# Order of VectorE's work in a Strassen-like gate/up stage: splits of later weights behind the products' sums, and the seam to the down projection

## The chip, the cores and the metric

One core of one Trainium2 chip. The metric is the device time of one execution in microseconds (us); a lower time is better. Engines: PE is TensorE, DVE is VectorE, ACT is ScalarE, POOL is GpSimd, SP is SyncE, which issues all DMAs.

## The reference

Input x of 2 x 512 x 512 passes through a Mamba-2 layer with a gated MLP, a layer norm, a BitLinear feed-forward with ternary weights, and a second layer norm. The change touches the gated MLP:

```python
h2 = rmsnorm(h, ln2_w)
mlp = silu(h2 @ gate_w.T) * (h2 @ up_w.T) @ down_w.T      # INTER = 1792, D_MODEL = 512
return res + mlp
...
def _bitlinear(x, w):
    scale = jnp.mean(jnp.abs(w))
    q = jnp.round(jnp.clip(w / (scale + EPS), -1.0, 1.0))
    return x @ (q * scale).T
```

## The kernel before

All products keep fp32 accuracy with single-pass matmuls: each operand is split into a high part (ScalarE copies it to the rounded type) and a low part (VectorE or GpSimd subtracts the high part from the original), and three products of parts are summed in PSUM.

Gate and up are computed for both batches together with seven products instead of eight (a 2x2 block scheme of the Strassen-Winograd kind). For each of 14 tiles f of 128 inner columns, PE runs six matmuls for each product: p6, then p4 of the tile before, p5, p7 and p3 (p1 and p2 of most tiles ran earlier, under the scan; for the tiles 11, 12 and 13 they are "fillers" within tiles 1, 3 and 5). VectorE forms the sums: line 1245 (p6: u_t), line 1251 (p5: v_t), line 1257 (p7: adds v_t, written to p5's PSUM bank), line 1263 (p3: c12), line 1269 (m1: silu(c12) times the sum, which frees p5's bank) and lines 1276 and 1279 (p4). PE's p4 waits for line 1257 (c22_ready). Lines 1105 and 1114 are VectorE's splits of weights for later: 1105 for a filler ("ga" loads), 1114 for a22 two tiles on ("gb" loads). ScalarE's silu of c12 is line 1000.

Then comes the down projection: for each of 14 tiles f PE multiplies act (split at line 1010 on ScalarE and line 1313 on VectorE) by the down weights (split at line 845 on ScalarE and line 1304 on VectorE, two tiles for each load "dn"), into four accumulators, the PSUM banks psB that p5's last tiles used.

Meanwhile VectorE quantizes the ternary weights of the feed-forward in halves (lines 1327 and 1329).

All weights pass through one buffer raw with three slots. SyncE issues the loads in the order of the list LOADS; load n waits until load n - 3 has been used by all its readers:

```python
for n, (kind, *at) in enumerate(LOADS):
    if n >= RAW_SLOTS:
        for used in raw_used(n - RAW_SLOTS):
            sp.wait_ge(*used)
...
if n in TERN:
    return [(tern_ready, TERN.index(n) + 1)]
```

Around the seam the list reads gb 13, ternary 2, dn 0, dn 1, dn 2, ternary 3, dn 3, ternary 4. Each engine walks the same written-out list SCHEDULE and carries out the part of each step that is its own, strictly in order. build_schedule writes it.

Of the kernel before, what the change touches and what calls it, by code (L numbers as in the profile page):

```python
# [37 lines left out]
FM = 1792 // P  # L38
# [10 lines left out]
def build_schedule():  # L49

    steps, loads = [], []

    def load(kind, *which):
        loads.append((kind, *which))
        return ("load", len(loads) - 1)
# [98 lines left out]
    def ternary():  # L154

        which = tern.pop(0)
        halves = 1 if which == ("qdn", FF // 2) and FF % 2 else 2
        return [load(*which)], [("quant", which, i) for i in range(halves)]

    filler = {1: NPRE, 3: NPRE + 1, 5: NPRE + 2}  # L160
    halves = []
    for f in range(FM):
        steps.append(("p6", f))
        if f >= 1:
            steps += [("m1", f - 1), ("p4", f - 1)]
        if f + 1 < FM:
            steps.append(("gsplit", f + 1))
        if f + 2 < FM:
            steps.append(load("gb", f + 2))
        if f == FM - 1:  # L170
            steps.append(load("dn", 0))
        if f + 1 in filler:
            steps.append(load("ga", filler[f + 1]))
        steps.append(("p5", f))
        if f == FM - 1:
            steps += [("act", 0, 0), ("act", 0, 1)]
        if f in filler:
            steps.append(("p1", filler[f]))
        steps.append(("p7", f))
        if f < NPRE:  # L180
            steps.append(("silu0", f))
        steps.append(("p3", f))
        if f in filler:
            steps.append(("p2", filler[f]))
        if sums:
            steps.append(load(*sums.pop(0)))
        if f == 7:
            steps.append(("scales",))
        if f in (8, 10, 12):
            loads_now, halves = ternary()  # L190
            steps += loads_now
        if f >= 8:
            steps.append(halves.pop(0))
    steps += [("p4", FM - 1), load("dn", 1), ("m1", FM - 1)]

    for f in range(FM):
        if f % 2 == 0 and f // 2 + 2 < FM // 2:
# [3 lines left out]
        if f % 2 == 0:  # L201
            loads_now, halves = ternary()
# [5 lines left out]
    for f in range(FM):  # L208
# [7 lines left out]
        if f in (4, 6, 8, 10, 12):  # L216
            loads_now, halves = ternary()
# [7 lines left out]
    for b in range(NB):  # L225
        for f in range(FF):
# [9 lines left out]
            if tern and f in (2, 4):  # L236
                loads_now, halves = ternary()
# [11 lines left out]


SCHEDULE, LOADS = build_schedule()
RAW_SLOTS = 3
DN_EARLY = 9
# [1438 lines left out]
```

## Time and profile before

| | |
|---|---|
| median of 3 runs | 496.98 us (496.71 to 497.38) |
| the profiled execution, its own time | 495.74 us |
| its span, first to last instruction | 494.0 us |
| PE busy | 472.2 us, 96% |
| VectorE busy | 318.7 us, 65% |
| ScalarE busy | 236.4 us, 48% |
| GpSimd busy | 215.5 us, 44% |
| mean granted TensorE clock | 0.996 |

The engines run side by side, so the busy times overlap. What lies between the span and the device time is start and end of the execution.

### The profile page before, as it was taken

The numbers are of one execution on the slowest core, as the hardware profiler recorded it, in microseconds if no ns is written. First come the engines' busy times: TensorE is split into PE (matmuls) and PEld (weight loads), VectorE is DVE, ScalarE is ACT, GpSimd is POOL, SyncE is SP. The second block draws the span as 40 slices with busy tenths as digits, with TensorE's granted clock in tenths as the row PEclk, the third lists the DMA queues.
The fourth block names the chain that finished last, engine by engine and source line by source line (L and its number), as shares of the span: only waits on it lengthen the run. The fifth ranks groups of instructions, "written<-read, shape, count | busy, mean of one in ns | idle before, by whom it ended". The sixth has DMA issues, their size and how long they took to land.

```text
span 494.0 us, 6223 instructions
## 1 busy us (share of the span) xinstructions
PE 472.2 (96%) x2104; PEld 375.8 (76%) x2104; DVE 318.7 (65%) x518; ACT 236.4 (48%) x444; POOL 215.5 (44%) x242
## 2 busy tenths in 40 slices
PE   8998999989989979999999899999999999999995
PEld 7776677766757868888788778888888888888884
DVE  3793786735788856777998889865957513411223
ACT  5887767776556667455343244233806430033200
POOL 5835476626773596767877000010004432133321
PEclk9999999999999999999999999999999999999998
DMA  7631022013202415342322257510300000200001
GB/s 244 204 108 49 37 86 65 21 40 110 83 26 85 158 56 192 130 161 95 129 97 81 79 198 227 171 45 2 127 21 1 0 0 1 85 2 0 2 14 71
DMA packets 14431, 40.80 MB, mean 83 GB/s; under 512 B 2368, under 2 KB 2368, under 8 KB 14400
## 3 DMA queue, kind: packets, MB, share of 16 engines
q1 hardware_dynamic: 14400, 40.41, 24.1%
q8 instruction: 17, 0.28, 0.2%
q14 instruction: 14, 0.11, 0.1%
HBM read 38.30 MB, written 2.10 MB: 82 GB/s over the span
## 4 chain that ended last, share of the span: by engine, by line
PE 78%; DVE 12%; issue 4%; ACT 3%; POOL 1%; POOLq 0%; DVEq 0%; ACTq 0%
PE psA L1619 8%; PE psA L1620 8%; PE psA L1408 6%; PE psA L1410 6%; PE psB L1629 4%; PE psB L1628 4%; PE psA L1414 3%; PE psA L1416 3%; PE psA L1598 3%; PE psA L1594 3%; PE psA L1597 3%; DVE xbc L1168 2%; PE psB L1594 2%; PE psB L1598 2%; PE psB L1597 2%
## 5 line engine op out<-in xcount | busy, mean ns | idle before, releaser
L1619 PE MATMUL psA<-xT_h,q_gu 128*128 128x512 f32 x176 | 70.1, 398 | 0.0
L1620 PE MATMUL psA<-xT_l,q_gu 128*128 128x512 f32 x176 | 69.1, 393 | 0.0
L669 POOL TENSOR_SCALAR var<-mv 128x1 f32<-128x1 f32 x16 | 4.9, 304 | 128.8 <-DVE mv L1060 128.7
L1031 ACT ACTIVATE gate_t<-psA 128x512 f32<-128x512 f32 x22 | 13.1, 597 | 75.1 <-PE psA L1620 75.1
L816 POOL TENSOR_TENSOR int_l<-prod_t,int_h 128x512 fp32r<-128x512 f32 x22 | 28.7, 1305 | 45.7 <-ACT int_h L1036 45.7
L1360 DVE TENSOR_TENSOR prod_t<-gate_t,psA 128x512 f32<-128x512 f32 x22 | 15.2, 689 | 51.7 <-PE psA L1620 48.6
L727 POOL TENSOR_TENSOR beta<-wsum,beta 128x512 fp32r<-128x512 f32 x28 | 36.1, 1310 | 25.0 <-ACT beta L892 25.0
L1619 PEld LDWEIGHTS psA<-xT_h,q_gu 128*128 128x128 f32 x176 | 33.1, 188 | 8.2
L1620 PEld LDWEIGHTS psA<-xT_l,q_gu 128*128 128x128 f32 x176 | 33.1, 188 | 7.4
L1629 PE MATMUL psB<-q_dn,int_l 128*128 128x512 f32 x88 | 34.3, 389 | 0.0
L1628 PE MATMUL psB<-q_dn,int_h 128*128 128x512 f32 x88 | 34.2, 389 | 0.0
L1000 ACT ACTIVATE c<-c 128x512 f32<-128x512 f32 x14 | 8.9, 633 | 51.1 <-DVE c L1263 51.1
L1396 PE MATMUL psA<-xT_h,win_h 128*128 128x512 f32 x80 | 32.7, 409 | 0.0
L1397 PE MATMUL psA<-xT_l,win_h 128*128 128x512 f32 x80 | 31.4, 392 | 0.0
L1168 DVE SCALAR_TENSOR_TENSOR xbc<-psA,convw_sb,xbc 128x511 f32<-128x511 f32 (+2 forms) x36 | 26.8, 746 | 0.8
L1329 DVE SCALAR_TENSOR_TENSOR q<-raw,scl,qtmp 128x512 fp8e4<-128x512 f32 x33 | 25.7, 779 | 1.2
L1010 ACT ACTIVATE act_hl<-act 128x512 fp32r<-128x512 f32 x28 | 16.9, 623 | 17.7 <-PE psB L1598 12.4
L1367 DVE SCALAR_TENSOR_TENSOR x<-psB,scl,x 128x512 f32<-128x512 f32 x8 | 6.0, 751 | 26.5 <-PE psB L1629 26.5
L1408 PE MATMUL psA<-xT_h,beta 128*128 128x512 f32 x56 | 22.4, 399 | 0.3 <-DVE act L1279 0.3
L1313 DVE TENSOR_TENSOR act_hl<-act,act_hl 128x512 fp32r<-128x512 f32 x28 | 19.1, 687 | 4.9 <-ACT act_hl L1010 4.9
L1410 PE MATMUL psA<-xT_l,beta 128*128 128x512 f32 x56 | 21.9, 391 | 0.0
L1401 PE MATMUL psA<-xT_h,win_l 128*128 128x512 f32 x80 | 21.9, 395 | 0.0
(251 smaller groups left out, 1359.1 us busy)
## 6 DMA issues: line engine op xcount, KB each, us to landing
raw<-in_f_gu_t SPq DMA_DIRECT2D x22, 512.0 KB, 3.5
raw<-in_w_gu_t SPq DMA_DIRECT2D x14, 512.0 KB, 4.1
raw<-in_f_dn_t SPq DMA_DIRECT2D x10, 512.0 KB, 3.3
raw<-in_w_gu_t SPq DMA_DIRECT2D x14, 256.0 KB, 2.7
raw<-in_w_dn_t SPq DMA_DIRECT2D x7, 512.0 KB, 3.3
raw<-in_w_in_t SPq DMA_DIRECT2D x5, 512.0 KB, 4.4
x<-in_hidden SPq DMA_DIRECT2D x8, 256.0 KB, 5.3
out<-x SPq DMA_DIRECT2D x8, 256.0 KB, 2.0
```

The lines of the kernel that those rows point to most:

```text
L727: nc.gpsimd.tensor_tensor(beta[:, f % 2, 1, cols], wsum[:, f % 2, cols], beta[:, f % 2, 0, cols].bitcast(F32), ALU.subtract).then_inc(gb_l ...
L816: nc.gpsimd.tensor_tensor(int_l[:, f, :], prod_t[:, n % 2, :], int_h[:, f, :].bitcast(F32), ALU.subtract).then_inc(int_ready, 1)
L1168: add = nc.vector.scalar_tensor_tensor(out=xbc[b][:, j, back:L], in0=bank_a(job)[:, 0:L - back], scalar=convw_sb[:, j, TAPS - 1 - back:TAP ...
L1329: last = nc.vector.scalar_tensor_tensor(out=q8[:, f, cols], in0=raw[:, n % RAW_SLOTS, cols], scalar=scl[:, 6 + w:7 + w], in1=qtmp[:, cols] ...
L1396: nc.tensor.matmul(ps, sh, mh, start=i == 0, stop=False)
L1397: nc.tensor.matmul(ps, sh, ml, start=False, stop=False)
L1408: nc.tensor.matmul(ps, weights[:, 0, chunk(k)], high[:, k, :], start=opens and k == 0, stop=False, skip_group_check=not opens)
L1410: nc.tensor.matmul(ps, weights[:, 0, chunk(k)], low[:, k, :], start=False, stop=False, skip_group_check=not opens)
L1619: nc.tensor.matmul(ps, w, seq(xT_h, k, b), start=k == 0, stop=False)
L1620: done = nc.tensor.matmul(ps, w, seq(xT_l, k, b), start=False, stop=k == KD - 1)
L1628: nc.tensor.matmul(ps, int_h[:, f, chunk(c)], q_dn[:, f, :], start=f == 0, stop=False)
L1629: done = nc.tensor.matmul(ps, int_l[:, f, chunk(c)], q_dn[:, f, :], start=False, stop=f == FF - 1)
```

## The change

The list of steps is written in another order within the seven products; no step is added or dropped. For every tile the sum of the fifth product stands ahead of the gb load's step. A filler's ga step moves from ahead of the fifth product to behind the third. In the last tile, act's first tile and the step of dn 0 move behind the seventh product, act's second tile behind the third product. At the end m1 comes ahead of p4 and of dn 1, and the last half of ternary weights 2 is quantized behind dn 1 instead of directly behind the third product. The order of the loads among themselves stays.

```diff
         if f + 1 < FM:
             steps.append(("gsplit", f + 1))
+        steps.append(("p5", f))
         if f + 2 < FM:
             steps.append(load("gb", f + 2))
-        if f == FM - 1:
-            steps.append(load("dn", 0))
-        if f + 1 in filler:
-            steps.append(load("ga", filler[f + 1]))
-        steps.append(("p5", f))
-        if f == FM - 1:
-            steps += [("act", 0, 0), ("act", 0, 1)]
         if f in filler:
             steps.append(("p1", filler[f]))
         steps.append(("p7", f))
         if f < NPRE:
             steps.append(("silu0", f))
+        if f == FM - 1:
+            steps += [("act", 0, 0), load("dn", 0)]
         steps.append(("p3", f))
+        if f == FM - 1:
+            steps.append(("act", 0, 1))
+        if f + 1 in filler:
+            steps.append(load("ga", filler[f + 1]))
         if f in filler:
             steps.append(("p2", filler[f]))
...
-        if f >= 8:
+        if 8 <= f < FM - 1:
             steps.append(halves.pop(0))
-    steps += [("p4", FM - 1), load("dn", 1), ("m1", FM - 1)]
+    steps += [("m1", FM - 1), ("p4", FM - 1), load("dn", 1), halves.pop(0)]
```

## Rows read from the trace of the kernel before

**Rows 1.** The page's first part: busy us, share of the span, instructions.

```profile
PE 472.2 (96%) x2104; PEld 375.8 (76%) x2104; DVE 318.7 (65%) x518; ACT 236.4 (48%) x444; POOL 215.5 (44%) x242
```

**Rows 2.** PE's waits from 176 to 494 us: total us, times, longest.

```profile
PE psA L1408 <- DVE psB L1257: 2.1, 2, 1.2
PE psB L1594 <- DVE act L1269: 1.2, 1, 1.2
...
```

**Rows 3.** Timeline at the first wait: start, duration (us), engine, line, operation.

```profile
183.09 0.39 PE L1416 MATMUL psA<-tT_h,beta 128*128 128x512 f32 x1
184.34 0.47 PE L1408 MATMUL psA<-tT_h,a 128*128 128x512 f32 x1 [0.86 <-DVE psB L1257]
...
189.96 0.40 PE L1408 MATMUL psA<-xT_h,beta 128*128 128x512 f32 x1
...
181.06 1.72 DVE L1105 TENSOR_TENSOR alpha<-raw,alpha 128x512 fp32r<-128x512 f32 x1
182.71 0.68 DVE L1251 TENSOR_TENSOR v_t<-psB,u_t 128x512 f32<-128x512 f32 x1
183.49 0.70 DVE L1257 TENSOR_TENSOR psB<-psA,v_t 128x512 f32<-128x512 f32 x1
...
186.81 0.69 DVE L1279 TENSOR_TENSOR act<-psA,act 128x512 f32<-128x512 f32 x1
```

**Rows 4.** Timeline of VectorE at the seam to the down projection.

```profile
279.48 1.22 DVE L1304 TENSOR_TENSOR dn_early<-raw,dn_early 128x1024 fp32r<-128x1024 f32 x1
...
281.21 1.28 DVE L1313 TENSOR_TENSOR act_hl<-act,act_hl 128x512 fp32r<-128x512 f32 x2
...
283.02 0.68 DVE L1263 TENSOR_TENSOR c<-psA,v_t 128x512 f32<-128x512 f32 x1
...
284.13 0.75 DVE L1329 SCALAR_TENSOR_TENSOR q<-raw,scl,qtmp 128x512 fp8e4<-128x512 f32 x1
...
286.25 1.22 DVE L1304 TENSOR_TENSOR dn_early<-raw,dn_early 128x1024 fp32r<-128x1024 f32 x1
287.38 0.68 DVE L1269 TENSOR_TENSOR act<-psB,c 128x512 f32<-128x512 f32 x1
289.28 1.23 DVE L1304 TENSOR_TENSOR dn_early<-raw,dn_early 128x1024 fp32r<-128x1024 f32 x1 [1.22 <-ACT dn_early L845]
290.42 0.69 DVE L1313 TENSOR_TENSOR act_hl<-act,act_hl 128x512 fp32r<-128x512 f32 x1
```

**Rows 5.** Timeline of PE, ScalarE and SyncE's queue at the same place.

```profile
281.62 0.40 PE L1416 MATMUL psA<-xT_h,beta 128*128 128x512 f32 x1
283.26 0.47 PE L1408 MATMUL psA<-tT_h,a 128*128 128x512 f32 x1 [1.24 <-DVE psB L1257]
...
288.12 0.50 PE L1594 MATMUL psB<-dn_early,act_hl 128*128 128x512 f32 x1 [1.21 <-DVE act L1269]
...
291.69 0.39 PE L1594 MATMUL psB<-dn_early,act_hl 128*128 128x512 f32 x1
...
283.73 0.63 ACT L1000 ACTIVATE c<-c 128x512 f32<-128x512 f32 x1 [5.22 <-DVE c L1263]
...
288.19 1.06 ACT L845 ACTIVATE dn_early<-raw 128x1024 fp32r<-128x1024 f32 x1 [2.87 <-DMA raw<-in_w_dn_t]
...
284.91 0.33 SPq L645 DMA_DIRECT2D raw<-in_w_dn_t  x1
```

**Rows 6.** Stretches: us, busy of five engines, granted clock, DMA share, GB/s.

```profile
2.00:3.00 1.00, 0.59 (x3) 0.59 (x4) 0.00 (x0) 0.06 (x1) 0.88 (x3) 1.00 0.76 285
4.00:5.00 1.00, 1.00 (x6) 1.00 (x5) 0.00 (x0) 0.95 (x4) 0.49 (x2) 1.00 0.71 207
6.00:7.00 1.00, 1.00 (x12) 1.00 (x11) 0.71 (x2) 0.13 (x1) 0.17 (x1) 1.00 0.78 233
490.00:491.00 1.00, 0.00 (x0) 0.00 (x0) 0.32 (x1) 0.00 (x0) 0.92 (x2) 0.66 0.00 0
```

**Rows 7.** Timeline of PE at the end of the span.

```profile
487.76 0.39 PE L1629 MATMUL psB<-q_dn,int_l 128*128 128x512 f32 x1
```

## The prediction

> **What bounds the kernel now.** I read the page first. TensorE (PE) is busy for 472.2 us, 96% of the span [rows 1], so a change of order on VectorE can only act through the moments in which PE stands still. The list of PE's waits comes next, from the first of the seven products to the end of the span [rows 2]: two waits for the sum that line 1257 writes, 2.1 us together, and one of 1.2 us for line 1269. Apart from one wait of less than 0.4 us near 246 us, that is all. After 288.12 us PE waits for nothing to the end of the span. So a delay or a gain at the start of the down stage reaches the end undiminished: nothing behind it has slack to swallow or to refill.
>
> The timeline at the first of these waits [rows 3] shows that the last matmul of the second tile's sixth product starts at 183.09 us, and the fourth product's first not before 184.34. The latter wants the sum of tile 0's seventh product (line 1257), which VectorE starts at 183.49, directly behind the fifth's sum (line 1251, 182.71). That one stood behind a split of 1.72 us at line 1105. Six matmuls start 0.23 us apart, a product takes 1.4 us, so the fifth product had been out since about 179.3: VectorE's order made the wait. The other two waits are of the same kind and stand at the seam to the down stage [rows 4, 5]: the split of the first down weights (279.48) and two splits of act (281.21) precede the last tile's seventh sum, and PE restarts at 283.26; then the split of the second down weights (286.25) precedes line 1269 (287.38), which frees the bank that the down product's fourth accumulator wants, and PE restarts at 288.12.
>
> The third thing to read is SyncE's row [rows 5]. It issues the third load of down weights (dn 2) at 284.91. The buffer raw has three slots, and this load takes the slot of ternary weights 2; their second half is read by line 1329, which runs 0.75 us from 284.13, to 284.88 [rows 4]. So this load waits for VectorE's quantization, and its place in VectorE's order sets when the load goes out. ScalarE takes the load up at 288.19, 3.28 us after its issue, VectorE splits it at 289.28, and only then comes act's split for tile 2, at 290.42, done at 291.11. PE starts tile 2 of down at 291.69. The margin is 0.6 us.
>
> **The change part by part.** No instruction is added or removed; PE's, GpSimd's and SyncE's orders of instructions stay as they are (the list of loads keeps its order), VectorE's and ScalarE's change.
>
> First part, tiles 0 to 12. The sum of the fifth product goes ahead of the split at line 1114, and the filler's split at line 1105, with ScalarE's copy that feeds it, goes behind the third product. For tile 0, the seventh product is out at about 180.7, and with line 1105 gone VectorE can start line 1257 at 181.06, where that split started. It ends by 181.8, before PE asks for it at 183.09 + 0.23 = 183.32. Gain: 184.34 - 183.32 = 1.02 us, and 0.08 more because the first matmul after a wait takes 0.47 us against 0.39 us: **1.1 us**. The split at line 1105 now waits for ScalarE behind the third product's silu, to about 184.0. It costs from 0.7 us (line 1251's size, the same 128x512) to 1.72 us, so it ends at 184.7 to 185.7. Queued behind it on VectorE are the next tile's u_t (0.6), m1 (0.6) and the two steps of p4 (0.7 and 0.7, line 1279 last): done between 187.4 and 188.4. For these PE waits with tile 1's third product, which would now start at 189.96 - 1.02 = 188.94. Hidden behind PE's products, with 0.5 us left at the dear end; without that cover it would cost 1 us. The filler's own product comes at about 186.1, also later than the split. The other two fillers (13 and the one before it) have the same pattern without a wait of before, so 0. The splits of line 1114 feed a product two tiles on: 0.
>
> Second part, tile 13. I keep the clock of before and subtract the 1.1 at the end. PE ends the seventh product at about 280.6 (six matmuls, 1.4 us, ahead of 282.0, where the last product ends). Line 1257 runs at once, to 281.4. PE wants it at 281.62 + 0.23 = 281.85, instead of 283.26: the second wait goes, 1.4 us. Then VectorE: first split of act 281.25, first down split 281.85, which holds it 1.13 us (279.48 to the next, less the later spacing), so the third product's sum at 283.0, as before (283.02). ScalarE's silu follows 0.7 later (283.73 before), and only behind it, by its new order, the copy for the second tile of act: 284.25 to 284.85. VectorE stands idle from 283.7 to 284.9. Then its second split of act, 284.9; m1 (line 1269) 285.5 to 286.2; p4's two steps 286.1 and 286.8; the second down split 287.4; the quantization 288.55, then line 1329 at 289.05 to **289.8**.
>
> What this does to PE is in two steps. The down product reaches its fourth accumulator at 281.85 + 1.4 + 9 x 0.23 = 285.3 and waits for m1 to 286.25: 1.9 us earlier than 288.12, and the first and second tile of down end at 289.8. Here the third tile should begin. But the load of dn 2 now goes out at 289.8 instead of 284.9, **4.9 us later**. With the same 3.28 us to ScalarE, 1.09 to VectorE's split, 1.14 to act's split and 0.69 for it, that is 293.1, 294.2, 295.35, 296.05. ScalarE's copy of act for tile 2 stands behind the down copy in its order, so it can't slip ahead. PE starts tile 2 at 296.15 instead of 291.69: **4.4 us later**, after standing still for 6.1 us; 0.1 more for the restart (0.50 against 0.39) makes 4.5. Queued behind on SyncE are the loads of ternary weights 3 and dn 3, which shift by as much, as does VectorE's later work; PE has shifted by nearly the same, so the next tiles keep their margins and cost nothing.
>
> Third part, the clock. The waits of [rows 2] are 1.2 us at most, and the mean clock stays at 0.996 over the span. What a longer pause does shows at the end of the span: the last matmul starts at 487.76 [rows 7], and in the stretch from 490 to 491 us the granted clock is 0.66 on average [rows 6]: it fell about 2.2 us after PE's last work, from 2.4 to 1.2 GHz. After 6.1 us of idling I expect the same fall. What a fall costs: at the start of the span PE runs transposes of one shape, 3 in 0.59 us, then 6 per us, and 12 per us in the stretch from 6 to 7 us [rows 6]; so half speed lasted between 2.6 and 4.6 us (the clock's column says 1.00 there, the rate doesn't). Half of that is lost: 1.3 to 2.3 us. I take **1.6 us**, a little under the middle, since 5.0 us is only the last moment at which the slow rate is seen; the term is an estimate. The Trainium skill (TensorE: Matmul & The Clock Gate, "What's actually happening") has the throttled state as the default, which activity releases; the row at the end of the span agrees. By that rule the time is 502.0 us, and 500.4 us if this pause is an exception to it.
>
> **Sum.** -1.1 + 4.5 + 1.6 = +5.0 us. The profiled execution took 495.74 us, of which 494.0 are the span and 1.7 lie around it; it would take 500.7. The median of the runs is 1.24 above it, so 496.98 + 5.0 = **502.0 us**.
>
> **The rivals.**
> A: the load is late as above, but the clock doesn't fall. For it: PE's waits of up to 1.2 us passed without a fall. Against it: the fall 2.2 us after the last matmul. -1.1 + 4.5 = +3.4: 500.4 us.
> B, on the other side: faster, because dn 2 isn't held by the quantization. This is one mechanism: the load goes out at 284.9 as before, and VectorE alone sets the pace. It would quantize to 289.8, split dn 2 to 290.9 and act to 291.5, and PE would start tile 2 at 291.6, as before. Left is the first wait, -1.1, perhaps -1.3: 495.8 us. Against it stands the issue 0.03 us behind line 1329's end [rows 4, 5]. It decides from the point where the load goes out less than 1.1 us later than before.
> C: no measurable change: part of the delay is caught up by something I took as fixed (a landing faster than 3.28 us, a shorter chain on VectorE), to within 1 us of before. It would need 3.4 us out of a chain of 11 us: 497 us.
> D: more than I forecast: a fallen clock for all of 4.6 us, or a second stall at tiles 4 or 6 of down, because three loads of 512 KB are now under way together: 503.5 us or more.
>
> **How the numbers follow.** The late load with the fallen clock has a chance of 0.64, A 0.17, D 0.08, B 0.06, C 0.05. About 1 us, 0.2%, is what a measurement of this kernel can tell from no change. Faster 0.06, same 0.05, slower 0.89. The range runs from A, 500.4 less 0.3 for the landing, to the dear end of the clock (2.3) with 1 us of uncertainty in the chain: 500.1 to 503.7.
>
> **What would show it.** In the profile after: no wait of PE near 182 us (if there is one, the first part is wrong); line 1257 for the last tile at about 279.5 and no wait for it; SyncE's load of dn 2 directly behind the quantization, at about 288.7; PE idle for about 6 us ahead of tile 2 of down, put down to line 1313; a granted clock under 1.00 in the few us behind it. The prediction is wrong if the load of dn 2 goes out early, if ScalarE copies act's tile 2 ahead of it, or if PE's waits later in down absorb something; in before there are none.

## The result, and the profile after

The changed kernel takes 502.71 us (median of 4 runs, 501.66 to 503.50) against 497.12 us before; the ratio is 1.0118 with a 95% interval of 1.0106 to 1.0130, which is +5.9 us (5.3 to 6.5). The prediction was 502.0 us, range 500.1 to 503.7.

The first part of the page, with PE 1% less busy in a longer span, and the clock's row in 40 slices, whose eights and seven name the slices in which the granted clock fell:

```profile
PE 477.2 (95%) x2104; PEld 380.1 (76%) x2104; DVE 313.5 (62%) x518; ACT 236.9 (47%) x444; POOL 214.6 (43%) x242
...
PEclk9998999999989999999999979999999999999999
```

PE's waits from 170 us on, to be laid beside [rows 2]:

```profile
PE psB L1594 <- DVE act_hl L1313: 6.2, 1, 6.2
PE psA L1408 <- ACT act L987: 1.7, 1, 1.7
PE psB L1594 <- DVE act L1269: 0.8, 1, 0.8
PE psA L1408 <- DVE act L1279: 0.3, 1, 0.3
```

Both waits for line 1257 are gone, the one for line 1269 has shrunk from 1.2 to 0.8 us, and one of 6.2 us has come up (the 1.7 and the 0.3 us stand in the kernel before too, the former ahead of the stretch of [rows 2]). The timeline shows where; first VectorE, ScalarE and SyncE, then PE:

```profile
182.58 0.69 DVE L1257 TENSOR_TENSOR psB<-psA,v_t 128x512 f32<-128x512 f32 x1
...
185.61 0.96 DVE L1105 TENSOR_TENSOR alpha<-raw,alpha 128x512 fp32r<-128x512 f32 x1 [1.22 <-ACT alpha L872]
...
281.03 0.70 DVE L1257 TENSOR_TENSOR psB<-psA,v_t 128x512 f32<-128x512 f32 x1 [0.48 <-PE psA L1416]
...
283.37 0.69 DVE L1263 TENSOR_TENSOR c<-psA,v_t 128x512 f32<-128x512 f32 x1
285.28 0.69 DVE L1313 TENSOR_TENSOR act_hl<-act,act_hl 128x512 fp32r<-128x512 f32 x1 [1.22 <-ACT act_hl L1010]
...
289.47 0.75 DVE L1329 SCALAR_TENSOR_TENSOR q<-raw,scl,qtmp 128x512 fp8e4<-128x512 f32 x1
294.59 1.23 DVE L1304 TENSOR_TENSOR dn_early<-raw,dn_early 128x1024 fp32r<-128x1024 f32 x1 [4.37 <-ACT dn_early L845]
295.73 0.69 DVE L1313 TENSOR_TENSOR act_hl<-act,act_hl 128x512 fp32r<-128x512 f32 x1
...
293.50 1.06 ACT L845 ACTIVATE dn_early<-raw 128x1024 fp32r<-128x1024 f32 x1 [7.31 <-DMA raw<-in_w_dn_t]
...
290.25 0.33 SPq L645 DMA_DIRECT2D raw<-in_w_dn_t  x1
...
184.65 0.39 PE L1416 MATMUL psA<-tT_h,beta 128*128 128x512 f32 x1
184.88 0.39 PE L1408 MATMUL psA<-tT_h,a 128*128 128x512 f32 x1
...
286.62 0.50 PE L1594 MATMUL psB<-dn_early,act_hl 128*128 128x512 f32 x1 [0.82 <-DVE act L1269]
...
289.97 0.39 PE L1598 MATMUL psB<-dn_early,act_hl 128*128 128x512 f32 x1
296.56 0.76 PE L1594 MATMUL psB<-dn_early,act_hl 128*128 128x512 f32 x1 [6.20 <-DVE act_hl L1313]
...
301.82 0.63 PE L1594 MATMUL psB<-dn_early,act_hl 128*128 128x512 f32 x1
302.24 0.50 PE L1597 MATMUL psB<-dn_early,act_hl 128*128 128x512 f32 x1
```

The two profiles can't be subtracted as they stand. The last matmul of the second tile's sixth product starts at 183.09 in [rows 3] and at 184.65 here, 1.56 us later, before anything changed could act. The stretches of the changed kernel say why: the granted clock fell twice in the part that is the same in both (the first three rows; the last four are of the down stage). Matmul by matmul, PE keeps within 0.2 us of the kernel before up to 47 us and falls back there, of which all but 0.3 us is taken back by 57 us; from 145.2 us on it falls back again.

```profile
44.00:48.00 4.00, 2.44 (x7) 1.56 (x8) 0.00 (x0) 3.98 (x7) 3.88 (x3) 0.81 0.02 4
48.00:52.00 4.00, 4.00 (x17) 2.93 (x16) 1.55 (x3) 2.17 (x4) 2.37 (x3) 0.77 0.40 131
145.00:150.00 5.00, 5.00 (x18) 3.91 (x18) 2.07 (x4) 3.72 (x10) 1.28 (x1) 0.66 0.01 5
295.00:296.00 1.00, 0.00 (x0) 0.00 (x0) 1.00 (x2) 0.59 (x2) 0.00 (x0) 0.82 0.68 270
296.00:297.00 1.00, 0.44 (x1) 0.47 (x2) 0.96 (x3) 0.14 (x1) 0.00 (x0) 0.50 0.25 78
301.00:302.00 1.00, 1.00 (x4) 0.81 (x3) 0.96 (x3) 0.00 (x0) 0.00 (x0) 0.50 0.91 360
302.00:303.00 1.00, 1.00 (x5) 0.81 (x4) 1.00 (x3) 0.29 (x1) 0.00 (x0) 0.77 0.87 152
```

The other three runs of this kernel have a mean clock of 0.991 to 0.992 against 0.985 in this one, so these two falls belong to this execution and not to the change; three of the 17 executions of the kernel before that ran beside the later experiments have 0.991 as well, where its others there have 0.996 to 0.998. Taking off the 1.56 us, the rows give the change's own account. The last tile's third sum starts at 283.37 - 1.56 = 281.81, against 283.02 in [rows 4]: 1.2 us gained in tile 0. SyncE issues dn 2 at 288.7 against 284.9 in [rows 5]: 3.8 us later, and 5.0 us later than it would be if only the 1.2 us gained had moved it. The third down tile starts at 295.0 against 291.69: +3.3, that is -1.2 and +4.5. And from 296.56 to 302.24 PE starts 13 matmuls 0.43 us apart instead of 0.23, at a granted clock of 0.50, which is 1.2 GHz: 5.7 us for 3.0 us of work, 2.7 us lost. The sum, +6.0 us, agrees with the measured ratio.

### The profile page after: what moved, and what is told of

Its sections match the earlier page's. It is cut to its first block, busy times and chain, and to the rows that moved or that the text cites. A ratio compares the mean times of both kernels' runs of the same rounds, so it can differ in the third digit from the quotient of the medians.

```text
span 501.8 us, 6223 instructions
## 1 busy us (share of the span) xinstructions
PE 477.2 (95%) x2104; PEld 380.1 (76%) x2104; DVE 313.5 (62%) x518; ACT 236.9 (47%) x444; POOL 214.6 (43%) x242
## 4 chain that ended last, share of the span: by engine, by line
PE 80%; DVE 10%; issue 4%; ACT 3%; POOL 1%; DMA 1%; POOLq 0%; DVEq 0%; ACTq 0%
PE psA L1619 8%; PE psA L1620 8%; PE psA L1408 6%; PE psA L1410 6%; PE psB L1629 4%; PE psB L1628 4%; PE psA L1414 3%; PE psA L1416 3%; PE psA L1594 3%; PE psA L1597 3%; PE psA L1598 3%; DVE xbc L1168 2%; PE psB L1594 2%; PE psB L1597 2%; PE psB L1598 2%
## 5 line engine op out<-in xcount | busy, mean ns | idle before, releaser
L1594 PE MATMUL psB<-dn_early,act_hl 128*128 128x512 f32 x36 | 15.5, 430 | 7.0 <-DVE act_hl L1313 6.2
```

The lines of the kernel that those rows point to most:

```text
L1594: nc.tensor.matmul(ps, act_high[c], high, start=f == 0, stop=False)
```

## The experiments

All ratios are to the kernel before, run in turn on the same chip; e1, e2, e4 and e6 shared a chip (before: 496.24 us), and e3, e5, e8 and e9 another (before: 496.61 us). The kernels are called by these short names below.

**Only the quantization back (e1).** This undoes one edit of the change: the last half of ternary weights 2 no longer stands at the very end.

```diff
-        if 8 <= f < FM - 1:
+        if f >= 8:
             steps.append(halves.pop(0))
-    steps += [("m1", FM - 1), ("p4", FM - 1), load("dn", 1), halves.pop(0)]
+    steps += [("m1", FM - 1), ("p4", FM - 1), load("dn", 1)]
```

> The changed kernel with one edit taken back: the last half of ternary weights 2 is quantized at the end of the last tile's list, ahead of m1, no longer behind the second down split. Theory L (the load of dn 2 waits for the quantization): it goes out about 1.8 us later than in the kernel before (the quantization still stands behind act's second split), PE's third down tile starts 1.3 us later, and with 1.1 us gained in tile 0 the time is 497.3 us, no fall of the clock. Rival V (VectorE's amount of work ahead of act's split for tile 2 sets the pace; the load is hidden): the same work still stands ahead of it, so 502 to 503 us.

Measured: 497.34 us, ratio 1.0020 (1.0011 to 1.0029), +1.0 us. Against the changed kernel's ratio that is 4.9 us less, so rival V falls, but it is 0.8 us above what theory L says. The timeline and three stretches of this kernel:

```profile
285.76 0.33 SPq L645 DMA_DIRECT2D raw<-in_w_dn_t  x1
...
286.39 0.50 PE L1594 MATMUL psB<-dn_early,act_hl 128*128 128x512 f32 x1 [2.00 <-DVE act L1269]
...
292.27 0.47 PE L1594 MATMUL psB<-dn_early,act_hl 128*128 128x512 f32 x1 [2.19 <-DVE act_hl L1313]
...
293.05 0.63 PE L1594 MATMUL psB<-dn_early,act_hl 128*128 128x512 f32 x1
```

```profile
292.00:293.00 1.00, 0.73 (x3) 0.67 (x4) 0.96 (x3) 0.98 (x2) 0.00 (x0) 1.00 0.44 102
293.00:294.00 1.00, 1.00 (x4) 0.76 (x3) 1.00 (x3) 1.00 (x3) 0.00 (x0) 0.51 0.97 397
296.00:297.00 1.00, 1.00 (x5) 0.79 (x4) 1.00 (x3) 0.00 (x0) 0.00 (x0) 0.78 0.96 209
```

dn 2 goes out at 285.8 and the third down tile starts 6.5 us later, much as it does in the changed kernel (290.25 to 296.56: 6.3) and in [rows 5] (6.8, of which 0.6 is margin). But at 293.0 us, 0.7 us after PE had set to work again, the granted clock fell to 0.50 and stayed there until after 296. "No fall of the clock" was the wrong half of the expectation: here two waits of 2.0 and 2.2 us, with 3.7 us of work between them (286.39 to 292.27 - 2.19), went ahead of a fall. Whether they caused it is what the next kernel asks.

**The same, with PE kept busy in its two waits (e8; the diff is against e1).** fill(n) is n transposes of 128x128 into a bank that is free by then.

```diff
+                    if n == 2:
+                        fill(15)
...
+                        if n == 0 and c == NC - 1:
+                            pe.wait_ge(*freed_a(("p6", FM - 1)))
+                            fill(14)
```

> The kernel of e1_quant_back with 14 and 15 more transposes on PE ahead of its two waits of 2.0 and 2.2 us at the start of down; they change no result. Theory C2 (in e1 the granted clock fell to 0.50 for 3.3 us behind these two waits, which costs 1.5 us): the restarts stay, the clock stays at 1.00 and the time is 1.2 us below e1's, 0.0 to 0.2% above before's on the same chip. Rival (the clock's fall has nothing to do with these waits, or is covered by VectorE's pace): as e1, 0.2% above before or more.

Measured: 496.63 us, ratio 1.0002 (0.9991 to 1.0013). The third down tile starts at 292.51, with 0.3 us of waiting ahead of it instead of 2.2, and the clock reads 1.00 in every stretch from 284 to 300 us. Against the ratio of e1 this is 0.9 us less, of 1.2 expected; the two intervals still overlap a little and were taken on two chips, so the times alone leave it close. The clock decides it: all twelve executions of this kernel have a mean clock of 0.996 to 0.999, ten of e1's eleven 0.994 to 0.995 and the last 0.987.

**The quantization in VectorE's gap (e2, the gap kernel).** It moves to directly behind the third sum, where VectorE stands idle for 1.2 us.

```diff
         if f == FM - 1:
-            steps.append(("act", 0, 1))
+            steps += [halves.pop(0), ("act", 0, 1)]
...
-    steps += [("m1", FM - 1), ("p4", FM - 1), load("dn", 1), halves.pop(0)]
+    steps += [("m1", FM - 1), ("p4", FM - 1), load("dn", 1)]
```

> The changed kernel with the quantization directly behind the third product's sum, in the 1.2 us in which VectorE waits for ScalarE's copy of act's second tile. Theory L: the load of dn 2 goes out as in the kernel before, the third down tile starts 0.5 us earlier than there, and with 1.1 us from tile 0 the time is 495.5 us. Rival V: VectorE has 1.2 us less ahead of act's split than in the changed kernel, so 501.5 us.

Measured: 494.88 us, ratio 0.9967 (0.9955 to 0.9980), -1.6 us. The same work stands ahead of act's split for tile 2 as in the changed kernel; only its order differs, and the time differs by 7.5 us. From its timeline:

```profile
283.79 0.33 SPq L645 DMA_DIRECT2D raw<-in_w_dn_t  x1
...
288.17 1.22 DVE L1304 TENSOR_TENSOR dn_early<-raw,dn_early 128x1024 fp32r<-128x1024 f32 x1 [0.61 <-ACT dn_early L845]
...
290.14 0.47 PE L1594 MATMUL psB<-dn_early,act_hl 128*128 128x512 f32 x1 [1.26 <-DVE act_hl L1313]
```

With the 1.56 us taken off the changed kernel's profile, its load goes out at 288.7 and its tile starts at 295.0: here both are 4.9 us earlier (at 183 us this profile lies within 0.1 us of the one before), and the clock stays at 1.00, which is the other 2.7 us. Theory L stands, rival V has fallen.

**The first part alone (e4)**, with the last tile and the seam as before (the diff is against the kernel before).

```diff
-        if f + 2 < FM:
-            steps.append(load("gb", f + 2))
         if f == FM - 1:
             steps.append(load("dn", 0))
-        if f + 1 in filler:
-            steps.append(load("ga", filler[f + 1]))
         steps.append(("p5", f))
         if f == FM - 1:
             steps += [("act", 0, 0), ("act", 0, 1)]
+        if f + 2 < FM:
+            steps.append(load("gb", f + 2))
...
         steps.append(("p3", f))
+        if f + 1 in filler:
+            steps.append(load("ga", filler[f + 1]))
```

> The first part alone: the fifth product's sum ahead of the gb split and the filler's split behind the third product; the last tile and the seam as in the kernel before. Expected: the wait of 0.9 us for line 1257 in tile 0 is gone, gain 1.1 us, 496.0 us. Rival: the later filler's split makes PE wait for line 1279 in tile 1 or the gain is eaten at the seam, where VectorE and the loads set the pace: 497.1 us.

Measured: 495.46 us, ratio 0.9980 (0.9969 to 0.9990), -1.0 us (0.5 to 1.5). Its list of waits from 176 us on has one wait for line 1257 left, the one at the seam, where [rows 2] have two:

```profile
PE psA L1408 <- DVE psB L1257: 1.2, 1, 1.2
PE psB L1594 <- DVE act L1269: 1.2, 1, 1.2
```

**The seam alone (e5)**, with the splits of tiles 0 to 12 where they were (the diff is against the changed kernel).

```diff
-        steps.append(("p5", f))
         if f + 2 < FM:
             steps.append(load("gb", f + 2))
+        if f + 1 in filler:
+            steps.append(load("ga", filler[f + 1]))
+        steps.append(("p5", f))
...
-        if f + 1 in filler:
-            steps.append(load("ga", filler[f + 1]))
```

> The seam alone: everything at the last tile and behind it as changed, but for the tiles 0 to 12 the splits stand where they stood before. Expected if the two parts add up: the changed kernel's +5.9 us and 0.8 to 1.1 us from the lost gain in tile 0, +6.8 us against before. Rival (the tile 0 gain is lost in the 6 us pause anyway, since the pace behind it is set by VectorE and the load): +5.9 us.

Measured: 503.15 us, ratio 1.0137 (1.0117 to 1.0158), +6.8 us (5.8 to 7.8). The size is the one expected, but the interval just reaches the rival's 5.9. The profile is sharper: in it the third down tile starts at 297.76, 1.2 us later than in the changed kernel's, and both have the same falls of the clock ahead of the stage, with the matmul of 184.65 at 184.66 here. So the gain of tile 0 does get through the pause. Not all of it lasts: the slow stretch of the clock ends at about the same time in both (302.8 and 302.5), so the kernel that restarts later runs less of its work in it, and at the fifth down tile the distance is 0.8 us (305.70 against 304.90).

**PE kept busy in the pause (e6).** The changed kernel with transposes ahead of the third down tile.

```diff
+                    if n == 2:
+                        pe.wait_ge(*freed_a(("p6", FM - 1)))
+                        for _ in range(50):
+                            nc.tensor.transpose(bank_a(("p6", FM - 1))[:, 0:P], ident[:], ident[:])
```

> The changed kernel with 50 more transposes of 128x128 on PE ahead of the third down tile, into a bank that is free by then; they change no result. They fill about 5.5 of the 6.2 us in which PE stands still. Theory C (the fall of the clock behind that pause costs 2.6 us: 13 matmuls at 0.43 us instead of 0.23): the restart stays where it is, the granted clock stays at 1.00 behind it, and the time is 500.2 us. Rival (the clock's fall is covered, since VectorE or the loads set the pace of the down tiles behind it): 502.7 us, as the changed kernel.

Measured: 500.11 us, ratio 1.0073 (1.0061 to 1.0086), +3.6 us. Against the changed kernel's ratio that is 2.2 us less, where 2.6 were expected. The stretches show PE at work and the clock held:

```profile
290.00:295.00 5.00, 5.00 (x48) 4.97 (x46) 0.96 (x1) 2.05 (x3) 0.00 (x0) 1.00 0.87 314
295.00:300.00 5.00, 4.20 (x20) 3.35 (x19) 4.93 (x9) 2.15 (x4) 0.00 (x0) 1.00 0.40 117
```

The third down tile starts at 296.01; at 183 us this profile lies 0.95 us behind the one before, so that is 295.1 in the clock of before, where the changed kernel has 295.0. PE restarts where it did, and only the clock differs. So the fallen clock is worth 2.2 us of the result by this comparison and 2.7 by the profile, and isn't covered by another engine's pace.

**Act ahead of the load (e3).** The gap kernel, and act's tile 2 ahead of the step of dn 2 on every engine (the diff is against the gap kernel).

```diff
     for f in range(FM):
+        if f == 0:
+            steps.append(("act", 0, f + 2))
         if f % 2 == 0 and f // 2 + 2 < FM // 2:
             steps.append(load("dn", f // 2 + 2))
-        steps.append(("act", 0, f + 2) if f + 2 < FM else ("act", 1, f + 2 - FM))
+        if f > 0:
+            steps.append(("act", 0, f + 2) if f + 2 < FM else ("act", 1, f + 2 - FM))
```

> The kernel of e2_quant_in_gap with act's tile 2 ahead of the step of dn 2 on every engine (ScalarE copies act before it waits for the load, VectorE splits it before dn 2). Theory L: the wait of 1.3 us for line 1313 ahead of the third down tile came from standing behind the load; it goes, and the time is 1.3 us below e2's, 2.7 us below before's. Rival (VectorE's amount of work is the bound here, so a wait of the same size comes up one or two tiles later): as e2, 1.4 us below before's.

Measured: 493.32 us, ratio 0.9939 (0.9924 to 0.9954), -3.0 us. Its waits from 176 us on (three lines of code further down, the same statements) have lost the one for act's split, and none has come up behind it:

```profile
PE psB L1597 <- DVE act L1272: 0.8, 1, 0.8
PE psA L1411 <- DVE act L1282: 0.3, 1, 0.3
```

**m1 ahead of act's second tile as well (e9).** Act's copy and split also stand ahead of the dn load's for every pair of down tiles (the diff is against the gap kernel).

```diff
-            steps += [halves.pop(0), ("act", 0, 1)]
+            steps += [halves.pop(0), ("m1", f), ("act", 0, 1)]
...
-    steps += [("m1", FM - 1), ("p4", FM - 1), load("dn", 1)]
+    steps += [("p4", FM - 1), load("dn", 1)]
...
+        steps.append(("act", 0, f + 2) if f + 2 < FM else ("act", 1, f + 2 - FM))
         if f % 2 == 0 and f // 2 + 2 < FM // 2:
             steps.append(load("dn", f // 2 + 2))
-        steps.append(("act", 0, f + 2) if f + 2 < FM else ("act", 1, f + 2 - FM))
```

> As e3_act_first, and m1 of the last tile ahead of act's second tile, and act's copy and split ahead of the dn load's for every pair of down tiles. Theory L: the last wait at the seam (0.8 us for line 1269) goes as well, 3.3 us below before's. Rival (VectorE is busy without a break here, so PE waits 0.5 us or more for the next split instead): as e3, 2.7 us below before's or less of a gain.

Measured: 493.51 us, ratio 0.9940 (0.9924 to 0.9956), -3.0 us. The wait for line 1269 is gone from the list, 0.2 us for line 1313 has come in its place, and the time doesn't tell this kernel from e3: 0.6 us is smaller than the interval. The trace does, for this place:

```profile
288.48 0.47 PE L1594 MATMUL psB<-dn_early,act_hl 128*128 128x512 f32 x1
...
291.71 0.47 PE L1594 MATMUL psB<-dn_early,act_hl 128*128 128x512 f32 x1 [0.25 <-DVE act_hl L1313]
```

These are the first matmuls of the third and the fourth down tile; e3 has them at 288.76 and 291.49, and its profile runs 0.2 us ahead of this one (the first down matmul at 282.20 against 282.43). So e9 starts the third tile 0.5 us earlier than e3 and the fourth at the same time: the gain is gone one tile on, where PE waits for line 1313 and VectorE has stood idle for only 0.2 us since 283. That is what the rival said. Both kernels are faster than either kernel of the comparison.

## Why the prediction was right

**The place of the cost.** The step on which it hung was that SyncE issues dn 2 only when the quantization has freed the slot. Expected at 288.7, measured at 290.25 - 1.56 = 288.7; from there 3.25 us to ScalarE (3.28 forecast), 1.09 to VectorE's split, 1.14 to act's. PE stood still for 6.2 us (6.1 forecast), and the delay of 4.5 us was met (4.5). The gap kernel shows that it was the load's place and not the amount of work, and the kernel kept busy measures this part without the clock: +3.6 us, where -1.1 + 4.5 = +3.4 had been forecast.

**The first part.** 1.1 us were forecast; the profile shows 1.2, and alone it measured 1.0 (0.5 to 1.5). The filler's split took 0.96 us, between the bounds of 0.7 and 1.72, and started at 184.05 in the clock of before, where 184.0 stood. Its cover held: no wait for line 1279 in tile 1.

**The second wait and the third.** The wait for the last tile's line 1257 went, and PE restarted behind m1 1.5 us earlier than in [rows 5] in the profile's own clock, but 3.1 us with the 1.56 taken off; 1.9 + 1.1 = 3.0 had been forecast. Neither gain could reach the end, since the third down tile waits for a chain that starts at the quantization. What they are worth once that chain is out of the way shows in e3: -3.0 us against the -1.0 of the first part alone.

**The clock.** The mechanism held: the granted clock fell in the pause, and PE worked at 1.2 GHz behind it. The size was too small: 1.6 us were taken from bounds of 1.3 to 2.3, and it cost 2.7 us in the profile and 2.2 us by the ratio of the kernel kept busy. Neither row from which the term was worked out carried over. The start of the span was read as 2.6 to 4.6 us at the slow rate, but [rows 6] have the full 12 transposes in the stretch from 6 to 7 us, so it was over by 6.0 and the upper bound is 3.6 us, a loss of 1.8. Nor is one execution a measure of it: in e4's profile only 7 of the same transposes fall into that stretch. Behind the pause the slow rate lasted for 5.7 us of work. And the end of the span had the fall 2.2 us after the last matmul, here it came 5.3 us after, only 0.9 us before PE set to work again: those rows gave that it would fall, not when. Of the 0.9 us between +5.0 and +5.9 us the clock is 0.6 us by the kernel kept busy and 1.1 us by the profile, so all or most of it. The 2.7 us also lie above the dear end of 2.3 for this term; that the time was within the range owes something to the 1 us allowed for the chain, which wasn't needed. The Trainium skill (TensorE: Matmul & The Clock Gate, "HAM oscillation — how this bites in real kernels") tells of a matmul kernel whose waits for DMA let the clock fall again and again; this case agrees, with one fall behind one late load.

**The rivals.** A (no fall) is refuted by the stretches, and the kernel kept busy, in which its condition was made true, measures close to its price. B and C needed the load to go out early or the chain to shrink by 3.4 us; neither happened. Of D's two halves the second stall at a later down tile didn't come: PE's list has no other wait. The first half, a clock fallen for all of 4.6 us, did come, and longer (5.7 us). Its price of 503.5 us was too high for that half alone: with 2.3 us for the clock the prediction's own sum gives 502.7 us.

## What to carry to other kernels

A read of a ring buffer is also a permission for a load. When an in-order engine's step is moved, look up which slot it frees and which transfer goes into it: 1.2 us of work moved behind some 5 us of other work made the kernel 7.5 us slower than the same 1.2 us in a gap of VectorE. Where an engine has to wait for a transfer, what doesn't need the transfer goes ahead of it in the list (1.3 us here). And a pause of PE is priced twice, once as a pause and once as a slower clock behind it; filling it with idle transposes gave back 2.2 us of 5.9.

## What the runs showed of the hardware

The granted clock doesn't fall at a fixed distance behind PE's last work: at the end of the span before it fell 2.2 us behind it [rows 6, 7], in the changed kernel 5.3 us (last matmul 289.97 to 290.36; the 0.82 of the stretch from 295 to 296 us puts the fall at 295.6), and in e1 only when PE had been at work again for 0.7 us, behind two pauses of 2 us. In the kernel before, two pauses of 1.2 us at the same place [rows 5] pass without a fall. With e8, which fills e1's two pauses and shows no fall, the runs say that pauses of about 2 us can bring one; they don't say from what length on. By the stretches the clock was back at 302.5 in the changed kernel, 5.9 us after PE had set to work, and at 296.4 in e1, 4.2 us after. So the price of a fall also depends on when PE comes back: the changed kernel and e5 met slow stretches of the same length, (295.6 to 302.5 and 296.0 to 302.8), and e5, which restarted 1.8 us after its fall instead of 0.9, lost 0.4 us less. And the clock can fall in a part of the kernel that is the same in both: the changed kernel's profiled execution lost 1.56 us there, which the profile before did not, so times of two profiles are to be laid over each other at a common instruction first.
